# Masks of the maxima's scores added by VectorE in PSUM in place of TensorE

## The reference, cut to what matters

```python
# attention a: 16 heads of 16; 40 OFFSETS: 0..32, 48, 64, 96, 128, 192, 256, 384
scores = stack([einsum('bhnd,bhnd->bhn', q, shift(k, delta)) for delta in OFFSETS], -1) * scale
scores = scores + pos_bias.T[None, :, None, :]
scores = where(arange(n)[:, None] < OFFSETS[None, :], -inf, scores)
alpha = softmax(scores, -1)            # then alpha-weighted shifted values, gate, Wout
# attention b: 16 heads of 16, causal
w = einsum('bhqd,bhkd->bhqk', q, k) / sqrt(dk)
w = softmax(where_causal(w, -1e10), -1)  # w * mask - 1e10 * (1 - mask)
```

## Time and profile before

| | us |
|---|---|
| median of 3 runs | 3341.37 (3329.47 to 3345.62) |
| the profiled execution | 3335.79 |
| its span, first to last instruction | 3333.9 |
| TensorE busy | 2755.0 (83%) |
| VectorE busy | 1653.6 (50%) |
| ScalarE busy | 1424.8 (43%) |
| POOL busy | 879.5 (26%) |

### The profile page before, as it was taken

One profiled execution on the slowest core, in us unless ns is written; L12 is line 12 of the kernel. 1 busy time (PEld: TensorE's weight loads), 2 busy tenths in 40 slices (PEclk: granted clock), 3 DMA queues, 4 the chain that ended last, 5 costly groups with the idle time before them and its releaser, 6 DMA issues. The chain is left out here.

```text
span 3333.9 us, 100742 instructions
## 1 busy us (share of the span) xinstructions
PE 2755.0 (83%) x45472; PEld 1602.5 (48%) x45472; DVE 1653.6 (50%) x2763; ACT 1424.8 (43%) x1409; POOL 879.5 (26%) x577
## 2 busy tenths in 40 slices
PE   3687888878888786699569999898989898997897
PEld 1455565655555565434334444444444444444343
DVE  3454444444444444610656666666666666674401
ACT  1354444444534443411125555555555555554401
POOL 3343434343434332000322222222222222210002
PEclk8789888889889888899779999999999999998998
DMA  8332323243333332379032222222222221312397
GB/s 199 78 102 70 98 65 98 75 106 83 97 80 83 81 84 52 120 297 401 22 88 58 58 58 59 58 58 58 58 59 58 52 63 43 65 31 98 139 415 267
DMA packets 234205, 344.58 MB, mean 103 GB/s; under 512 B 113972, under 2 KB 142840, under 8 KB 217400
## 3 DMA queue, kind: packets, MB, share of 16 engines
q1 hardware_dynamic: 208552, 310.40, 32.1%
q10 hardware_dynamic: 25232, 27.83, 3.6%
HBM read 266.54 MB, written 69.24 MB: 101 GB/s over the span
## 5 line engine op out<-in xcount | busy, mean ns | idle before, releaser
L1375 DVE TENSOR_REDUCE b_tops<-b_slot 128x8 f32<-128x1024 f32 x576 | 680.1, 1219 | 334.1 <-PE b_slot L1224 171.0
L1417 ACT ACTIVATE b_probs<-b_slot 128x1024 f32<-128x1024 f32 x576 | 583.0, 1023 | 523.5 <-PE b_slot L1232 371.6
L515 POOL COPY a_q_far<-a_q_near 96x1024 bf16<-96x1024 bf16 x128 | 259.1, 2053 | 300.9 <-PE a_slot L592 216.0
L1174 POOL TENSOR_SCALAR_AFFINE_SELECT b_probs<-b_probs 128x1024 f32<-128x1024 f32 x128 | 139.8, 1093 | 724.2 <-ACT b_probs L1417 724.2
L1252 PE MATMUL b_outT_ps<-b_probs,b_v 128*17 128x128 f32 (+3 forms) x4608 | 318.5, 384 | 6.2 <-ACT b_probs L1417 5.5
L1232 PE MATMUL b_slot<-b_q_stack,b_k_stack 99*128 99x512 bf16 (+3 forms) x1280 | 274.5, 321 | 42.8 <-DVE b_tops L1375 32.1
L901 ACT ACTIVATE a_k_far<-a_k_near 96x1024 bf16<-96x1024 bf16 x128 | 258.4, 2068 | 99.7 <-DMA a_k_near<-parts_near_dram 89.1
L1232 PE MATMUL b_slot<-b_k_stack,b_q_stack 96*128 96x512 bf16 (+3 forms) x1280 | 266.7, 323 | 30.9 <-DVE b_tops L1375 20.6
L795 DVE TENSOR_TENSOR a_probs<-a_slot,a_bias_k 128x1024 f32<-128x1024 f32 x128 | 154.4, 1217 | 140.0 <-PE a_slot L592 139.8
L864 ACT ACTIVATE a_probs<-a_probs 128x1024 f32<-128x1024 f32 x128 | 133.3, 1052 | 208.8 <-DVE a_probs L795 190.4
L804 DVE TENSOR_REDUCE a_tops<-a_slot 128x16 f32<-128x1024 f32 x128 | 156.1, 1221 | 104.2 <-PE a_slot L592 103.4
(11 more groups left out here) (224 smaller groups left out, 4259.8 us busy)
## 6 DMA issues: line engine op xcount, KB each, us to landing
f_w_ring<-in_L_ffn_w_dram SPq DMA_DIRECT2D x128, 1024.0 KB, 9.3
parts_near_dram<-a_parts ACTq DMA_DIRECT2D x96, 256.0 KB
parts_dram<-b_parts SPq DMA_DIRECT2D x96, 256.0 KB
a_k_near<-parts_near_dram SPq DMA_DIRECT2D x128, 128.0 KB, 2.9
b_k_stack<-parts_dram SPq DMA_DIRECT2D x64, 256.0 KB, 6.7
a_q_near<-parts_near_dram SPq DMA_DIRECT2D x64, 192.0 KB, 2.9
b_q_stack<-parts_dram SPq DMA_DIRECT2D x32, 384.0 KB, 4.6
values_dram<-a_v_stage SPq DMA_DIRECT2D x16, 544.0 KB
```

The costliest lines, as they stand in the source:

```text
L515: pool.tensor_copy(q_far[far][0:QK_ROWS, h, :].rearrange("p (r a) -> p r a", r=LINKS), q_near[near][0:QK_ROWS, h, :].rearrange("p (a r) -> ...
L1375: ins = dve.tensor_reduce(out, src, AX.X, ALU.max)
L1417: act.activation(probs_of(b, g, u, h)[:, :], slot_of(step)[:, :], ACT.Exp).then_inc(taken_act, 1)
```

## The change

In the band, the two products that write the table are gone; TensorE writes only the 32 x 32 corner of keys before the first, and the score products start their regions anew. VectorE then adds the table to the slot in place, as two adds over 128 x 512 each, waits for them, and reduces. In the dense attention the mask products of the diagonal unit are gone and VectorE adds the mask in place, as one add over 128 x 1024, before the reduction. Both count on a new semaphore that the two attentions share, and VectorE's reduction waits for it. The wait for the band's tables moves from TensorE to VectorE. In the first expert layer the add to the output's bias moves behind the last copies of `mergedT`, and the semaphore for it is gone.

```diff
@@ band_attention, TensorE, step mx
-                        if (b, g, h) == (0, 0, 0):
-                            pe.wait_ge(bias_in, 16 * 12)
                         pe.wait_ge(turned_q, turns)
                         pe.wait_ge(turned_k, turns)
                         dst = slot_free(step)
-                        for kind in range(2):
-                            pe.matmul(dst[:, 512 * kind:512 * (kind + 1)], ident16[:, :],
-                                      bias_q[kind][:, HG * g + h, :].unsqueeze(1).to_broadcast([P, NT, 64]), start=True, stop=False,
-                                      skip_group_check=True)
-                        pe.matmul(dst[:, 0:64], ident16[:, :], before_first[:, :], start=False, stop=False, skip_group_check=True)
-                        products(dst, slice(0, QK_ROWS), h % 2, q, k, False, False).then_inc(filled, 1)
+                        pe.matmul(dst[0:BLK, 0:BLK], ident16[:, 0:BLK], before_first[:, 0:BLK], start=True, stop=True, skip_group_check=True)
+                        products(dst, slice(0, QK_ROWS), h % 2, q, k, False, True).then_inc(filled, 1)
@@ band_attention, VectorE, step mx
+                            if (b, g, h) == (0, 0, 0):
+                                dve.wait_ge(bias_in, 16 * 12)
+                            for far in range(2):
+                                scores = src[:, 512 * far:512 * (far + 1)].rearrange("p (t c) -> p t c", c=64)
+                                dve.tensor_tensor(scores, scores, bias_q[far][:, HG * g + h, :].unsqueeze(1).to_broadcast([P, NT, 64]),
+                                                  ALU.add).then_inc(mx_masked, 1)
+                            dve.wait_ge(mx_masked, 2 * count("mx", "mx", b, g, h))
                             ins = dve.tensor_reduce(tops[:, h, :, :].rearrange("p k t -> p (k t)"),
                                                     src[:, :].rearrange("p (t c) -> p t c", c=64), AX.X, ALU.max)
@@ dense_attention, TensorE, steps S and mx, u == 0
-                            for c in range(2 if kind == "mx" else 0):
-                                pe.matmul(dst[:, 512 * c:512 * (c + 1)], ident16[:, :], later[:, :].unsqueeze(1).to_broadcast([P, 4, P]),
-                                          start=True, stop=False, skip_group_check=True)
                             for tile in range(NT):
                                 mine = slice(P * tile, P * tile + P)
-                                ins = pe.matmul(dst[:, mine], own[0:rows, h, mine], other[0:rows, h, mine], start=kind == "S", stop=True,
-                                                skip_group_check=True)
+                                ins = pe.matmul(dst[:, mine], own[0:rows, h, mine], other[0:rows, h, mine], start=True, stop=True)
@@ dense_attention, VectorE, step mx
+                            if u == 0:
+                                masked_before = MX_BAND + HG * (b * G + g) + h
+                                dve.tensor_tensor(src, src, later[:, :].unsqueeze(1).to_broadcast([P, NT, P]), ALU.add).then_inc(mx_masked, 1)
+                                dve.wait_ge(mx_masked, masked_before + 1)
                             ins = dve.tensor_reduce(out, src, AX.X, ALU.max)
@@ ffn, VectorE, setup of the dense constants
-                        dve.wait_ge(through_out, 1)
-                        dve.tensor_tensor(dense["o_bias"][:, :], bank[3][:, 0:D], dense["o_bias"][:, :], ALU.add)
...
                             dve.tensor_copy(mergedT[:, kd, :, 4 * gq:4 * gq + 4],
                                             bank[2][:, c0:c0 + P].rearrange("p (b e) -> p e b", e=NE)).then_inc(merged_ready, 1)
+                    if beside:
+                        dve.tensor_tensor(dense["o_bias"][:, :], bank[3][:, 0:D], dense["o_bias"][:, :], ALU.add)
```

More of the change, by code:

```diff
@@ L227, in pair_of, with band_attention @@
     return n // (2 * G), n // 2 % G, n % 2
-def band_attention(nc, x, x_sb, stats, ident, w, scratch, x_biased):
+def band_attention(nc, x, x_sb, stats, ident, w, scratch, x_biased, mx_masked):
     BY_TOKEN, BY_RESIDUE = 4, 3
@@ L236, in band_attention @@
     for name, kinds in {"filled": BY_DVE + BY_ACT, "taken_dve": BY_DVE, "taken_act": BY_ACT, "qk": ("q", "k"), **{kind: (kind,) for kind in (
-            "S", "PV", "ote", "z", "mred", "gmul", "fparts", "mrow", "part0", "rest1", "part1", "part2", "store2", "turn", "mt", "vin", "vout", "xb")}}.items():
+            "S", "PV", "ote", "z", "mred", "gmul", "fparts", "mrow", "part0", "rest1", "part1", "part2", "store2", "turn", "mt", "mx", "vin", "vout", "xb")}}.items():
         for step in seq:
@@ L1042, in dense_constants, with dense_attention @@
             "ident16": sb("ident16", [P, P], BF16), "later": sb("later", [P, P], BF16)}
-def dense_attention(nc, x_sb, stats, ident, w, scratch, x_biased):
+MX_BAND = 2 * B * H
+def dense_attention(nc, x_sb, stats, ident, w, scratch, x_biased, mx_masked):
     seq = dense_schedule()
@@ L1559, in ffn @@
             if beside:
-                weights_in, mask_steps, wide_ready, through_out = (ssem(n) for n in ("weights_in", "mask_steps", "wide_ready", "through_out"))
+                weights_in, mask_steps, wide_ready = (ssem(n) for n in ("weights_in", "mask_steps", "wide_ready"))
                 dense, wd = beside
@@ L1650, in _ @@
                         for kd in range(KD):
-                            ins = pe.matmul(bank[3][:, 0:D], dense["v_wide"][:, kd, :], dense["wout"][:, kd, :], start=kd == 0, stop=kd == KD - 1)
-                        ins.then_inc(through_out, 1)
+                            pe.matmul(bank[3][:, 0:D], dense["v_wide"][:, kd, :], dense["wout"][:, kd, :], start=kd == 0, stop=kd == KD - 1)
                     pe.wait_ge(merged_ready, 2)
@@ L2031, in build @@
     with (nc.sbuf_tensor("x_sb", [P, B * NT, D], F32) as x_sb, nc.sbuf_tensor("ident", [P, P], F32) as ident,
-          nc.sbuf_tensor("stats", [P, B * NT, 6], F32) as stats, nc.semaphore("x_biased") as x_biased):
-        band_attention(nc, a["L0_attn_a_x"], x_sb, stats, ident, attn_a, scratch, x_biased)
+          nc.sbuf_tensor("stats", [P, B * NT, 6], F32) as stats, nc.semaphore("x_biased") as x_biased, nc.semaphore("mx_masked") as mx_masked):
+        band_attention(nc, a["L0_attn_a_x"], x_sb, stats, ident, attn_a, scratch, x_biased, mx_masked)
         with ExitStack() as dense:
@@ L2036, in build @@
             ffn(nc, x_sb, stats, ident, experts, scratch, "f1_", beside=(constants, attn_b))
-            dense_attention(nc, x_sb, stats, ident, constants, scratch, x_biased)
+            dense_attention(nc, x_sb, stats, ident, constants, scratch, x_biased, mx_masked)
         ffn(nc, x_sb, stats, ident, experts, scratch, "f2_", out)
```

## The result

The changed kernel takes 3540.5 us (median of 4 runs, 3537.6 to 3543.6) against 3337.9 for the kernel before on the same chip: ratio 1.0608, 95% interval 1.0578 to 1.0638. It is slower by some 200 us; the forecast was 3490 in a range to 3570.

A forecast was written before the change was run, and what follows sets the result against it. TensorE was taken as the fuller engine, but waiting in stretches for VectorE's reductions to free PSUM slots. Dense queue 102, prologue 4, dense clock 37 and band 10 sum to 153 us, giving 3490 us, range 3405 to 3570.

The forecast's parts named there:

- Dense, the queue: Dense attention: VectorE's adds delay its freeing of three PSUM slots, 3.3 us in each of 31 groups, 102 us.
- the replay: Dense attention: one group's starts recomputed with a 1.22 us add per masked maximum; all queues end 3.3 us late.
- Dense, the clock: Dense attention: TensorE's clock falls behind the masks in three groups of four, 1.6 us each: 37 us, ends 0 and 99.
- Prologue: First dense group, maxima alone with VectorE back to back: four adds less the earlier first fill, 4 us.
- Band: Band attention: replay of one group per kind g, mean +0.33 us, times 31: 10 us, ends -69 and +78.
- The late maxima: Band attention: later maxima end some 2 us later, inside the 8 us VectorE waits for `fp`.
- o_bias: Add to the output bias (0.42 us) moved behind the merged copies: nothing, ends -0.4 and +0.4.
- B: Dense attention: the clock does not come back within a group, 99 us in place of 37: 3552, chance 0.17.
- D: Band attention pays its upper end, 68 us more: 3558, chance 0.10.
- A: Whole kernel: the forecast itself, 3490 us, chance 0.45.
- C: Dense attention: cheap add of 0.91 us and no clock loss: 3415, chance 0.20.
- E: Both attentions: delay taken back in each group, only TensorE's work counts, -53 dense and -69 band: 3215, chance 0.05.

The follow-up runs named there:

- dense_late: dense_only with three of each group's four masked maxima put later, to places 8, 12 and 16 of 18: 3499.6 us, 1.0459.
- dense_fill2: dense_only with extra TensorE products, overwritten afterwards, ahead of diagonal maxima 1 to 3 and the next unit's first maximum: 3462.2 us, 1.0345.
- dense_only: Only the dense attention's half of the change (and the moved output-bias add), band as in the kernel before: 3496.9 us, 1.0458.
- band_none: band_only without VectorE's adds, so no engine adds the table to the maxima's scores: 3347.3 us, 0.9998.
- band_only: Only the band's half of the change, dense attention as in the kernel before: 3380.1 us, 1.0108.
- band_keep: band_only with TensorE's table products kept and overwritten by the score products: 3401.8 us, 1.0172.
- dense_spread: dense_only with the masked maxima of a group at places 1, 5, 9 and 13 instead of four in a row: 3452.0 us, 1.0339.
- none_spread: Changed kernel without VectorE's table and mask adds in both attentions, diagonal maxima at places 1, 5, 9 and 13: 3315.0 us, 0.9905.

## Why the prediction came out as it did, point by point

**Where the difference lies.** The change cost 203 us, 50 more than the forecast's 153: 13 of them in the dense half alone (156 for 143), 29 in the band alone (39 for 10), and 8 that the halves do not show apart.

**Dense, the queue.** Right: 102 us forecast, 31 x 3.5 = 108 shown at full clock. The add cost what the row of an add out of PSUM said (1.225 for 1.22), the period was 2.40, and every start up to n1 lay within 0.07 us of the replay. One sentence of it is too weak: that VectorE has slack after the first stretch is true of its busy time, but dense_late, with three of the four masks moved there, still pays 2.8 us a group at full clock.

**Dense, the clock.** A fall behind the masks was right; that the 37 us are near what was measured is in part luck. dense_fill2 took most of the falls away and gave back 35 to 39 us; the dense stage of dense_only grew by 162 us (first to last exponential, 1476.5 for 1314.7), which leaves 53 beside the queue's 108. So the term lies between 35 and 53, far below 99. But it is made up otherwise than forecast. In place of falls of 3.2 us in three groups of four, the clock fell in every group of the changed kernel, for 6.8 to 13.7 us (21.6 in the first); and in place of half of that time, about 0.15 of it was lost: a group with a fall of 6.8 us took 46.2 us in dense_only, for 45.1 with none in dense_fill2. The two errors nearly cancel. Why so little of it counts is not shown; TensorE was busy in some 260 of the 303 us, so 130 could have been lost.

The Trainium skill ("TensorE: Matmul & The Clock Gate", section "A second HAM failure mode: psum-queue depth-cycling") said that throughput suffers from the clock's going up and down as PSUM tiles are cycled. The changed kernel's windows agree, with a fall in each of the 31 groups; the page names no price, and the larger end that the forecast set for it, 99 us, was not reached.

**Prologue.** 4 us forecast; from VectorE's first instruction on the maxima to the first exponential it is 32.0 us for 27.7, less the earlier first fill: right.

**Band.** This term failed: 10 us forecast, 39 measured alone. Three steps of it were wrong. The relief: the replay gave back 0.5 us for masks gone from TensorE in g=0 and g=1 and 0.4 in g=2, but by itself it is worth nothing (band_none, 0.9998), and the granted clock fell with it; "I add nothing for it" stood where most of the 102 us came back as slower products. Whether the relief would have counted at the old clock is not shown: TensorE also stood idle for longer (266 us to the last x, for 214 to 238 in the eight profiles whose band is as before). The late maxima: "some 2 us later, inside the 8 us in which VectorE waits for `fp`" looked at VectorE alone; their slots are what the projections want (the wait of 1.31 us above). And the adds cost 1.38 and not 1.25 us. From one `fp` to the next, groups got longer in all four kinds, by 2.3, 1.2, 0.7 and 2.1 us (means of five batches, band_only less before; in the order g = 0 to 3), where +0.8, +0.8, -0.4 and +0.1 were forecast; the 0.7 is hardly more than the scatter among versions whose band is untouched. In the same batches TensorE's waits for the maxima's reductions grew by 3.1, 1.3, 0.6 and 3.0 us a group. So the groups grew where these waits did, and most of the miss is in g = 3, where the projections' wait of 1.31 us is, and in g = 0. How the 39 us divide into waits and clock stays open even so: no run held the band's clock up without adding work to TensorE, and band_keep, which added it, did not bring the clock all the way back.

**o_bias.** Costed at nothing, and not seen apart; the stretch between the stages is about as long as before.

**Rivals.** By its number the result, 3540, is nearer to B (3552) and D (3558) than to A (3490), but neither is the cause: with B the dense half alone would be +205 and it is +156; with D the band would be +78 and it is +39. C fell with its two parts: the add was not cheap and the clock did fall. E, the other side, fell in the band, where the relief counted for nothing; in the dense stage TensorE's relief is worth 1.1 of 1.7 us a group, but VectorE's adds take 4.7.

**What would show it.** Adds of 1.2 and 0.65 us: 1.225 and 0.691. S(1,1) 14 us after the first S: 15.4 with the fall, 14.3 without. TensorE's waits: 141 us in the two lines, for 51 in the one. The clock below 0.98, falls behind the masks: 0.89, and there. The band longer by no more than 20 us: wrong, 48 in the profile.

## What to carry to other kernels

An engine that frees PSUM slots can be on the path though it looks idle: here, with three slots and 1.2 us to read each, of 4.85 us added to VectorE in a group 4.7 reached the end in one order and 2.7 in another (dense_spread less none_spread), though it had been idle for a third of the stage. Price such a move by replaying the slots' order, and look up everyone who takes a slot behind the longer reader, projections too. Do not count TensorE's relief at its face value in a stage that is not at full clock: in the band 102 us of products less changed nothing, and the granted clock fell with them.

## What was not expected of the hardware

Taking products away from TensorE lowered its granted clock over the whole band: 0.88 before, 0.81 with the table left out and nothing added anywhere (band_none):

```profile
110.00:1319.00 1209.00, 962.78 (x30216) 698.20 (x30217) 538.72 (x798) 535.89 (x411) 468.83 (x281) 0.81 0.33 83
```

To the band's last addition to x TensorE is busy for 994 us there, with 102 us of products gone, and for 1007 in the kernel before (1019 to 1038 in the seven versions whose band is untouched, at a clock of 0.84 to 0.86). In the dense stage, products whose results are overwritten held the clock up (303 us at half clock to 50), and dense_fill2 is 35 to 39 us faster than dense_only though it does more.
